# A decoder block on one core: the delta rule solved and run per half of the sequences, its second half inside the first mixture

## The reference, cut to what matters

```python
q, k, v = silu(causal_dwconv(x @ W, taps))          # 4 taps, per channel
q, k = l2norm(q), l2norm(k)                         # per head
inv = -(kb @ k.T) * strict_lower                    # 32x32 blocks, 4 in a sequence and head
for i in range(1, 32):
    inv[i, :] += inv[i, :] @ inv
inv = inv + eye
u, w = inv @ v, inv @ kb
# scan over the 4 blocks of a sequence and head:
attn = q_i @ k_i.T * lower_incl
u2 = u_i - w_i @ S
o_i = q_i @ S + attn @ u2
S = S + k_i.T @ u2
# four sources: short filter (5 taps), long filter (64 taps), delta output o, v
stats = [head_stats(t) for t in (short, long, delta, v)]   # mean, var, mean |x|, l2 per head
p = softmax(gelu([x, stats] @ Wg1) @ Wg2); o = mixture of the four by p
o = rmsnorm(o * sigmoid(gelu([x, stats of o and v] @ Wog1) @ Wog2)) @ Wo
x = layernorm(x + o)
```

## Time and profile before

| what | value |
|---|---|
| median of 3 runs | 499.55 us (497.66 to 502.07) |
| the profiled execution's own time | 501.34 us |
| its span | 499.5 us |
| TensorE busy | 388.5 us (78%) |
| VectorE busy | 321.0 us (64%) |
| ScalarE busy | 151.8 us (30%) |
| GpSimd busy | 37.5 us (7%) |
| mean granted TensorE clock | 0.83 |

### The profile page before, as it was taken

One profiled execution on the slowest core, in us unless ns is written; L12 is line 12 of the kernel. 1 busy time (PEld: TensorE's weight loads), 2 busy tenths in 40 slices (PEclk: granted clock), 3 DMA queues, 4 the chain that ended last, 5 costly groups with the idle time before them and its releaser, 6 DMA issues.

```text
span 499.5 us, 8308 instructions
## 1 busy us (share of the span) xinstructions
PE 388.5 (78%) x2952; PEld 279.2 (56%) x2952; DVE 321.0 (64%) x1050; ACT 151.8 (30%) x255; POOL 37.5 (7%) x76
## 2 busy tenths in 40 slices
PE   0979997969961999947155499897998879887992
PEld 0645664759831999932033355655566555564662
DVE  1043675778999532567834685657987688877635
ACT  1233242223551111233111234222543234413330
POOL 6000000007930000000000000000000000000000
PEclk9989999589955555575555879989999989999998
DMA  7470101197419200000001000000020000000000
GB/s 253 106 190 12 31 5 17 29 287 209 124 51 172 41 3 3 3 0 1 0 1 43 1 21 1 1 22 0 2 63 8 15 0 21 0 0 1 22 2 21
DMA packets 48305, 22.23 MB, mean 45 GB/s; under 512 B 17768, under 2 KB 47632, under 8 KB 48016
## 3 DMA queue, kind: packets, MB, share of 16 engines
q1 hardware_dynamic: 31760, 13.40, 11.0%
q10 hardware_dynamic: 16512, 8.39, 6.2%
HBM read 18.64 MB, written 3.15 MB: 44 GB/s over the span
## 4 chain that ended last, share of the span: by engine, by line
PE 47%; DVE 32%; issue 9%; DMA 6%; ACT 3%; SPq 2%; DVEq 0%; ACTq 0%; POOL 0%
PE bank L459 9%; PE bank L701 5%; PE bank L723 5%; PE bank L693 5%; PE bank L735 4%; PE bank L441 4%; DVE prod L1428 4%; DVE inv L1430 3%; DVE as_t L1408 2%; PE bank L494 2%; DVE as_t L1230 2%; DVE nt L1140 2%; DVE nt L1141 2%; DVE as_t L1221 2%; DVE sm L1142 2%
## 5 line engine op out<-in xcount | busy, mean ns | idle before, releaser
L701 PEld LDWEIGHTS bank<-w_sb,as_t 128*128 128x128 f32 x512 | 61.3, 194 | 23.1 <-issue 18.9
L701 PE MATMUL bank<-w_sb,as_t 128*128 128x128 f32 x512 | 64.2, 281 | 5.0 <-ACT as_t L1000 5.0
L1000 ACT ACTIVATE as_t<-bank,cb 128x512 f32<-128x512 f32 x64 | 43.3, 686 | 73.9 <-PE bank L693 58.6
L693 PE MATMUL bank<-as_t,w_sb 128*128 128x512 f32 x128 | 65.0, 634 | 0.0
L459 PE MATMUL bank<-wtap,xc_pad 128*128 128x384 f32 x128 | 47.8, 520 | 6.0 <-DVE wtap L1155 6.0
L1408 DVE SCALAR_TENSOR_TENSOR as_t<-bank,as_t 128x128 f32<-128x128 f32 x128 | 36.0, 343 | 23.4 <-PE bank L701 21.1
L723 PE MATMUL bank<-vb,early 32*32 32x32 f32 x512 | 29.9, 236 | 11.4 <-DMA early<-inverses 11.4
L441 PE MATMUL bank<-ident,as_t 128*128 128x128 f32 (+1 forms) x64 | 12.1, 319 | 34.1 <-DVE as_t L1230 15.7
L459 PEld LDWEIGHTS bank<-wtap,xc_pad 128*128 128x128 f32 x128 | 25.0, 203 | 23.7 <-DVE wtap L1155 6.4
L723 PEld LDWEIGHTS bank<-vb,early 32*32 32x32 f32 x512 | 28.2, 151 | 13.6 <-issue 12.8
L693 PEld LDWEIGHTS bank<-as_t,w_sb 128*128 128x128 f32 x128 | 23.4, 202 | 19.0 <-issue 17.7
(11 more groups left out here) (220 smaller groups left out, 632.9 us busy)
## 6 DMA issues: line engine op xcount, KB each, us to landing
toep<-taps_long ACTq DMA_DIRECT2D x8, 1024.0 KB, 7.0
toep<-x SPq DMA_DIRECT2D x8, 256.0 KB, 2.9
early<-x SPq DMA_DIRECT2D x4, 256.0 KB, 4.4
w_sb<-w SPq DMA_DIRECT2D x1, 1024.0 KB
w_sb<-w SPq DMA_DIRECT2D x2, 512.0 KB
blocks<-as_t SPq DMA_DIRECT2D x16, 64.0 KB, 2.0
early<-blocks SPq DMA_DIRECT2D x1, 1024.0 KB, 6.2
toep<-ctx_in SPq DMA_DIRECT2D x4, 256.0 KB, 3.6
```

What stands on the lines that cost most here:

```text
L693: pe.matmul(ps[4 + half][:, :], w1_sb[:, e, half * 128:half * 128 + 128], x2_c.rearrange("p b t -> p (b t)"), start=True, stop=True).then_ ...
L701: last = pe.matmul(bank(6 + e % 2)[:, b, :], hid[:, e % 2, half, b * L:(b + 1) * L], w2_sb[:, e, half, :], start=(half == 0), stop=(half = ...
L1000: act.activation(hid[:, e % 2, half, :], ps[4 + half][:, :], ACT.Relu, bias=c_of("b1", 2 * e + half)).then_inc(s["hid_ready"], 1)
```

## The change

Six edits, made together:

1. **Products and masks.** `products(g, 0)` now makes the key products of all four sequences and `products(g, 1)` the query products: 16 matmuls of 128 columns each, where there were 8 of 256. ScalarE copies the key products out unmasked (`keep_products`, 4 activations a group); VectorE masks the query products alone (4 operations a group, after `norms`). TensorE waits for the first before it writes the second into the same banks, and for the last masks before it begins the long filter.
2. **Blocks and solve per half** (groups 0 and 1, groups 2 and 3). Each half's blocks are gathered in a DMA of their own, one block on each partition, and solved by VectorE alone, with all rows; GpSimd solves nothing. The first half's columns 0 to 7 stand before `norms(3)`, 8 to 11 before the last masks, 12 to 30 behind them; the second half follows.
3. **Inverses and recursion per half.** Two round trips to DRAM, each with its half's solve; the second stands behind the loads of `xt`, `xa` and `c_g`. The first half's recursion stands between the pieces of the short filter of group 2 and chunks 6 and 7 of the long one. `u` is gone: results go to `vb` in place.
4. **The second recursion stands inside the first mixture**, on TensorE, ScalarE and VectorE.
5. **Sums.** Those of v are made in the projections (`square_v`, `v_sums`), the others for one half at a time. `source_moments` then takes the four sources of a half together, 16 operations on 128 columns. GpSimd's copies for groups 0 and 1 need the first half's alone.
6. **Roots in 8 operations**: two rounds with other constants, the second of a higher order.

```diff
 def rsqrt(y, a, n):
     own(dve.tensor_scalar(y.bitcast(I32), a.bitcast(I32), -0.5, RSQRT_GUESS, ...))
-    for i in range(3):
-        own(... t = y * y); own(... t = t * -0.5 * a); own(... y = (t + 1.5) * y)
+    own(... t = y * y); own(... t = t * -1.0 * a); own(... y = (t + ROOT_START) * y)
+    own(... t = y * y); own(... t = t * K * a); own(... t = (t + ROOT_A) * t); own(... y = (t + ROOT_B) * y)
@@ SP
-            sp.wait_ge(blocks_out, 16 * NG * NC)
-            sp.dma_start(blk[:, :, :, :].rearrange("p a j i -> p (a j i)"),
...
+            blocks(0)
+            blocks(1)
+            gather_blocks(0)
+            blocks(2)
+            blocks(3)
+            sp.wait_ge(s["gram_ps"], 2 * H * NG + credit["gram_ps"])
+            gather_blocks(1)
...
+            spread_inverses(0)
             sp.wait_ge(s["fir_ps"], CHUNKS)
             sp.dma_start(xt, x[0:G].rearrange("b t c -> t b c")).then_inc(xt_in, 16)
             sp.dma_start(xa, x[0:G].rearrange("b t c -> t b c")).then_inc(xa_in, 16)
             sp.dma_start(c_g, ctx_in[0:G].rearrange("b t c -> t b c")).then_inc(ctx_loaded, 16)
-            sp.wait_ge(s["solved"], 2)
...
+            spread_inverses(1)
@@ TensorE, products
-                for b in (2 * r, 2 * r + 1):
+                for b in range(G):
                     for h in range(H):
+                        if b == 0 and r == 1:
+                            pe.wait_ge(s["keys_kept"], g * H + h + 1)
-                                            kq_c[rows, b, :, :].rearrange("p k t -> p (k t)"), start=True, stop=True)
+                        product = pe.matmul(ps[4 + h][:, b * L:(b + 1) * L], kh_c[rows, b, :], kq_c[rows, b, r, :],
...
+            pe.wait_ge(s["gram_kept"], H * NG + credit["gram_kept"])
@@ ScalarE
+            def keep_products(g):
+                for h in range(H):
+                    act.wait_ge(s["gram_ps"], g * 2 * H + h + 1 + credit["gram_ps"])
+                    act.activation(rows_of[:, bass.ds(g * G, G), h, 0, :], bank(4 + h), ACT.Copy
+                                   ).then_inc(s["keys_kept"], 1)
@@ VectorE, projections
+            for g in (1, 2):
+                v_sums(g - 1)
                 gate_sums(g)
                 norms(g)
+                mask_products(g - 1)
+            v_sums(2)
+            dve.wait_ge(blocks_in[0], 16)
+            solve(0, 0, 8)
+            gate_sums(3)
+            norms(3)
+            mask_products(2)
+            solve(0, 8, 12)
+            mask_products(3)
+            solve(0, 12, CH - 1)
+            v_sums(3)
@@ VectorE, after the projections
+            dve.wait_ge(blocks_in[1], 16)
+            solve(1, 0, 18)
+            subtract_solved(1, 0)
+            subtract_solved(1, 1)
+            solve(1, 18, 24)
+            subtract_solved(2, 0)
+            subtract_solved(2, 1)
+            solve(1, 24, CH - 1)
+            subtract_solved(3, 0)
+            subtract_solved(3, 1)
+            source_sums(0, 0, 0, 1)
+            source_sums(1, 0, 8, 2)
+            dve.wait_ge(s["fir_ps"], CHUNKS)
+            keep_delta(0)
+            keep_delta(1)
+            source_sums(2, 0, 0, 3)
+            source_moments(0)
             rotate_keys(0)
...
+            source_sums(0, 1, 8, 4)
+            subtract_solved(1, 2)
+            subtract_solved(1, 3)
...
             mixture(0)
+            subtract_solved(2, 2)
+            subtract_solved(2, 3)
             mixture_stats(0)
-            source_moments(2, G, B)
+            source_sums(1, 1, 8, 5)
+            subtract_solved(3, 2)
+            subtract_solved(3, 3)
             gated(0)
             x1_norm(0)
+            keep_delta(2)
+            keep_delta(3)
+            source_sums(2, 1, 8, 6)
+            source_moments(1)
```

More of the change, by code:

```diff
@@ L76, in decoder_kernel @@
         flip = sb("flip", [128, 128])
-        masks = sb("masks", [128, 2, L])
+        causal = sb("causal", [128, L])
         tie = sb("tie", [128, 2, E, E])
@@ new lines, in solve_block @@
+            def solve_block(n, g):
+                half, i = g // HG, g % HG
+                at = (half * NC + n) * HG + i
+                rows = slice(CH * n, CH * n + CH)
+                if n == 0:
+                    pe.wait_ge(inverse_in[half], 16 * NC)
+                    if half:
+                        pe.wait_ge(s["delta_ready"], i + 1)
+                else:
+                    pe.wait_ge(s["r_ready"], (half * (NC - 1) + n - 1) * HG + i + 1)
+                    pe.wait_ge(s["u_ready"], at - HG + 1)
+                for r in range(GP):
+                    last = pe.matmul(ps[6 + i][rows, r * DH:(r + 1) * DH], inv_t[rows, GP * g + r, :],
+                                     vb[rows, GP * g + r, :], start=True, stop=True)
+                last.then_inc(s["d_ps"], 1)
@@ new lines, in apply_solved @@
+            def apply_solved(n, g):
+                half, i = g // HG, g % HG
+                rows = slice(CH * n, CH * n + CH)
+                pe.wait_ge(s["u_ready"], (half * NC + n - 1) * HG + i + 1)
+                if n > 1:
+                    pe.wait_ge(s["r_ready"], (half * (NC - 1) + n - 2) * HG + i + 1)
+                elif half:
+                    pe.wait_ge(s["oc_ready"], i + 1)
+                for r in range(GP):
+                    last = pe.matmul(ps[4 + i][rows, r * DH:(r + 1) * DH],
+                                     as_t[0:CH * n, GP * g + r, 0, rows], vb[0:CH * n, GP * g + r, :],
+                                     start=True, stop=True)
+                last.then_inc(s["a_ps"], 1)
@@ new lines, in outputs @@
+            def outputs(g):
+                half, i = g // HG, g % HG
+                pe.wait_ge(s["u_ready"], (half * NC + NC - 1) * HG + i + 1)
+                pe.wait_ge(s["r_ready"], (half * (NC - 1) + NC - 2) * HG + i + 1)
+                for r in range(GP):
+                    last = pe.matmul(ps[4 + i][r % H * DH:r % H * DH + DH, r // H * L:(r // H + 1) * L],
+                                     vb[:, GP * g + r, :], as_t[:, GP * g + r, 1, :], start=True, stop=True)
+                last.then_inc(s["o_ps"], 1)
@@ L569, in xat @@
+            solve_block(2, 1)
+            fir(6)
+            fir_transposed(6)
+            apply_solved(3, 0)
+            apply_solved(3, 1)
+            fir(7)
+            fir_transposed(7)
+            solve_block(3, 0)
+            solve_block(3, 1)
+            v_transposed(3)
+            outputs(0)
+            outputs(1)
+            short(3, 0, 2)
+            outputs_transposed(0)
+            outputs_transposed(1)
+            short(3, 2, 4)
             def xat(g):
@@ L780, in step @@
+            st2_transposed(0)
+            solve_block(2, 2)
+            solve_block(2, 3)
+            output_gate(0)
+            apply_solved(3, 2)
+            apply_solved(3, 3)
+            output_z(0)
+            solve_block(3, 2)
+            solve_block(3, 3)
+            ont(0)
+            outputs(2)
+            outputs(3)
+            wo(0)
+            outputs_transposed(2)
+            outputs_transposed(3)
+            pe.wait_ge(s["delta_ready"], NG)
             def step(g, experts_left):
@@ new lines, in solve @@
+            def solve(half, first, end):
+                for j in range(first, end):
+                    n, m = CH - 1 - j, j + 1
+                    p = prod[:, 0:m * n].rearrange("p (c i) -> p c i", c=m)
+                    own(dve.tensor_tensor(out=p, in0=blk[half][:, j, j + 1:].unsqueeze(1).broadcast_to([128, m, n]),
+                                          in1=wide(inv[:, half, 0:m, j], n), op=ALU.mult))
+                    own(dve.tensor_tensor(out=inv[:, half, 0:m, j + 1:], in0=inv[:, half, 0:m, j + 1:], in1=p,
+                                          op=ALU.subtract))
+                if end == CH - 1:
+                    dve.sem_inc(s["solved"], 1)
@@ L1279, in source_moments @@
[L1279 to L1284 removed]
+                seqs, pairs = slice(half * B // 2, (half + 1) * B // 2), slice(half * HP, (half + 1) * HP)
+                rows = src[:, seqs, k, :]
```

561 lines of the change are left out of this document (288 added, 273 removed).

## The result

The changed kernel measured 497.44 us (median of 15 runs, 491.29 to 502.16), the kernel before 500.76 (15 runs): a ratio of 0.9878, with a 95% interval of 0.9836 to 0.9920. It is 1.2% faster, where 2.3% was forecast (488 against 499.55). The profiled execution took 498.03, its span 496.3.

The account below looks back on a forecast made before the run. It took 54 us of saturated TensorE, then a 48 us mixture chain, then steps chained between TensorE and VectorE. -6.1 to the rotation and -6.1 in the steps gave 489.1 from 501.34; less 1.8, 487.5, rounded to 488 (range 467 to 503).

Parts of the forecast that it names:

- The 15 others: In the steps: 15 late roots on VectorE's chain lose two operations each, -6.1 us (-3 if half is hidden).
- The roots' price: Two operations fewer per root: 0.41 us in the steps; 0.16 and a gap of 0.04 per operation.
- Up to the statistics: From the start through the first recursion: statistics done at 193.0 us, where they were done at 224.7.
- The masks: End of the projections: last masks at 103.1 us for 98.35, with +2.1 for products, -0.4 roots, +3.1 copies.
- The solve's columns 12 to 30: First half's solve behind the masks: 38 operations, 3610 elements, 14.9 us, to 118.0.
- The inverses' trip: First half's inverses to DRAM and back: 7.8 us plus 3.1 for the filter's loads beside it, landing at 128.9.
- rival C: First inverses queue behind 1 MB loads on both ways, coming at 149.0, 17.5 us after TensorE: 505 us; chance 0.08.
- three at 1.1: First recursion's 14 calls: three at clock 1.00, 1.1 us each, and eleven at 1.84, together 23.5 us.
- The first mixture: Statistics to the queries' rotation, with the second recursion inside: 74.2 us where it was 48.6, +25.6.
- The exponential's +6.8: In the first mixture: the exponential starts behind two copies and its table load, 7.6 us after the logits for 0.8.
- the pairs' terms: In the first mixture: call pairs of 3.7 us lengthen the chain, +2.9 to +3.1 at each of five links.
- Rival A: Clock stays at 1.00 through the first recursion, long matmuls between its calls: -16.7 us, to 471; chance 0.20.

Follow-up runs that it names:

- the second profile: The changed kernel run once more with no edit, against the kernel before: 497.85 us, ratio 0.9833.

## Why the prediction was wrong

**The step that failed** is the one on the steps: "The 15 others lose two operations each: 15 x 0.41 = -6.1". It took the steps for a chain whose time falls by what VectorE no longer does. They became 5.1 us longer, 11.2 off, and this is more than the whole miss (498.0 for 489.1 in the profiled execution). Of the 11.2 steps 2 and 3 have 5.5 (59.3 and 59.2 for 57.7 and 55.3 without the stall, ten operations ahead), and the first step 5.8 (60.8, where 56.6 less four roots is 55.0). The runs show what stood in the place of the first part; the second is explained only in part.

- *The roots' price was about right.* Where the loop has no stall (ten operations ahead), steps 2 and 3 and the tail take 57.7, 55.3 and 52.0 for 59.1, 57.3 and 53.2: 4.6 us less, where thirteen roots should give 5.3. The first step, with its low clock, shows none of it.
- *The stall.* Shorter roots made a step's code 10 operations shorter, and moved the loop to a place where the jump back costs 3.1 + 1.8 us of standing still and 17 packets of instructions for 12, three of them around the stall. It appears with the roots alone, goes with the old roots, with the loop written out, and with ten operations ahead. The Trainium skill, "Runtime: NRT & Kernel Launch", section "Instruction fetch mechanics", says that a taken branch whose target isn't in the current two pages forces a fetch before execution goes on. The packets inside the stall, and none around the jump where there is no stall, agree with it; which parts of the code lie in those pages no view shows. I hadn't weighed it, and counted removed instructions only by their time.
- *The clock.* TensorE runs dry behind the stall, and step 3 gets half clock for 11 us: in the second profile 6.6 us on top of 3.9. In the first step the clock was at 0.50 for 26 us instead of 10, +4.2 with four shorter roots in it (the first step has no `finish`). It fell in a hole of TensorE, of 4.94 us behind the second half's sums, as in the kernel before in one of 5.54; with the sums moved away it fell in one of 7.01 at `x2_norm`. What of the 5.8 us is the clock and what the sums' place isn't isolated.

**Up to the statistics** the prediction said 193.0, and 193.2 was measured, by luck: six of the later profiles, the same up to there but for the roots in one, have 187.2 to 189.0, and in the first terms cancel. The masks end 5.6 us earlier than forecast (97.5 for 103.1): 32 records for 16 and the four copies cost nothing on the path. The solve's columns 12 to 30 took 15.0 for 14.9. The inverses' trip took 21.8 for 10.9: rival C's mechanism was there in good part in this profile, if not to its price, and cost only 2.7 us at the start (134.2 for 131.5), as TensorE wasn't there before 128.5. In the later ones TensorE began between 128.9 and 131.7 and didn't wait for the inverses. The calls ran at 1.81 from the first on, for three at 1.1; from their start to the statistics it was 59.0 us for 61.5, which gives the 2.7 back.

**The first mixture.** 71.8 us from the statistics to the rotation for 74.2. The exponential's +6.8 was +6.6; of the pairs' terms only the sum was tested, by the recursion in a row: 8.4 us longer in this stretch, 5 to 7 in the whole, for 6.5.

**Rival A** did not come true in the change itself, and its price had about the right size: -16.7 for the clock at 1.00 in the first recursion, and 14 to 18 us came when two loads were held (statistics 12.9 us earlier than in the second profile of the changed kernel, 2.5 by the earlier start and 10.4 behind it, by the clock). The prediction took the 50 us at 0.50 as evidence against full clock in the recursion. They show that small matmuls don't bring it up, and say nothing on whether a mixture with the filter's pieces keeps it. There the rule of the Trainium skill that was set against the trace ("TensorE: Matmul & The Clock Gate", "Why this matters for your kernels") held in its part on gaps: a hole of 5.66 us put back took the clock away. In seven profiles it fell without a hole, so that being busy wasn't enough; how the two loads come into it stays open.

**The size.** With the stall gone the change is worth 3.5 to 3.7% (0.9655 and 0.963), more than the forecast's 2.3%; with it, 1.2%. There the rotation comes at 258.4 and 259.2, 8 to 9 us ahead of the forecast's 267.2, so the sum was off in two directions. It also has a slip that decides nothing: 489.1 less 1.8 is 487.3, not 487.5.

## What to carry to other kernels

Instructions that are taken away from a looped engine move its code: look after each such edit at the loop's jump back for idle time that waits for nothing, and at the packets of the instruction queue, before the edit is judged; a few operations ahead of the loop, or the loop written out, may be worth more than the edit. Ask of every transfer on the path what else is in flight and when it is needed: two loads of 1 MB, not wanted for another 15 us and more, cost 14 to 18 us, by way of TensorE's clock. And a hole ahead of dense TensorE work is to be priced with its clock, not by its length: one of 5.7 us cost 16 to 17.5.

## What was not expected of the hardware

- The same loop, same length, with its code ten VectorE operations further on: no stall instead of 3.3 + 1.8 us, 12 packets on the instruction queue instead of 17, and none instead of three around the jump back.
- Small matmuls (32x32) with pieces of the filters between them kept the clock at 1.00 for 18 us with TensorE 96% busy, and did not raise it from 0.50 in 34 us at 97%; small matmuls alone did not in 54 at 99.7%.
- One half's inverses took 6.6 us to write and 15.0 to read beside loads of 1 MB in the first profile (6.8 and 8.4 with the last two held; in six later profiles with the loads in flight at most 11.2 to read); before, both halves' together took 10.4.
